# A graph network on one core: last passes with one span of 128 nodes per eight tiles, first pass with three bfloat16 parts side by side in one matmul

## What is computed

```python
h = jnp.maximum(_layernorm(x, axis=-1), 0.0)
x = x + _L0_gnn_ref(h, edge_index, edge_weight)      # segment_sum(h[src] * w, dst)
h = jnp.maximum(_layernorm(x, axis=-1), 0.0)
x = x + _L1_gnn_ref(...)                             # gate MLP per edge, summed by src
h = jnp.maximum(_layernorm(x, axis=-1), 0.0)
x = x + _L2_gnn_ref(h, edge_weight1, src, dst)       # edge softmax over dst, summed by dst, elu
h = jnp.maximum(_layernorm(x, axis=-1), 0.0)
x = x + _L3_gnn_ref(h, edge_weight, edge_index)      # segment_sum(x[src] * w, dst), twice
```

## Time and profile before

| | us |
|---|---|
| median of three timed runs | 12126.67 (12122.02 to 12133.5) |
| span of the profiled execution | 14505.6 |
| POOL busy | 9272.0 (64% of the span) |
| PE busy | 6101.2 (42%) |
| DVE busy | 4404.3 (30%) |
| ACT busy | 3763.8 (26%) |

### The profile page before, as it was taken

How to read it: one execution, slowest core, us unless ns; L and a number is a source line. 1 busy time by engine, 2 the same in 40 slices (tenths; PEclk the granted TensorE clock), 3 DMA queues, 4 the chain that set the end, 5 groups by cost and what they waited for, 6 DMA issues and landing times. The chain is left out here.

```text
span 14505.6 us, 217117 instructions
## 1 busy us (share of the span) xinstructions
PE 6101.2 (42%) x41742; PEld 4794.2 (33%) x41743; DVE 4404.3 (30%) x18474; ACT 3763.8 (26%) x13496; POOL 9272.0 (64%) x8348
## 2 busy tenths in 40 slices
PE   4444444444555555552333333233333333333333
PEld 2222122123444444442333333233333333333333
DVE  4444444445444444443111111211111111111111
ACT  2444444443222222221111111111111111111111
POOL 5555555555888888884666666566666666666665
DMA  4333333334455555542111111111111111111111
GB/s 115 101 102 100 97 96 95 94 96 66 62 61 61 61 61 62 61 61 47 16 16 16 16 16 16 20 16 16 16 16 16 16 22 16 16 16 16 16 16 21
DMA packets 805018, 671.16 MB, mean 46 GB/s; under 512 B 417876, under 2 KB 663828, under 8 KB 802727
## 3 DMA queue, kind: packets, MB, share of 16 engines
q0 software_dynamic: 452736, 234.14, 14.8%
q1 hardware_dynamic: 349659, 430.53, 11.3%
q10 hardware_dynamic: 2588, 6.12, 0.1%
HBM read 562.94 MB, written 107.13 MB: 46 GB/s over the span
## 5 line engine op out<-in xcount | busy, mean ns | idle before, releaser
L725 POOL DMA_INDIRECT table<-table,idx x4992 | 4900.3, 982 | 3003.1 <-issue 1544.4
L801 PE MATMUL psum_acc<-table 128*128 128x48 f32 (+1 forms) x12288 | 2854.8, 416 | 5083.8 <-DVE acc L765 2683.5
L801 PEld LDWEIGHTS psum_acc<-table 128*128 128x128 f32 x12288 | 2697.3, 329 | 5241.3 <-issue 5241.3
L1071 POOL DMA_INDIRECT sums<-rows,idx x1664 | 2620.6, 1575 | 577.2 <-issue 435.1
L504 POOL DMA_INDIRECT rows<-table,idx x1668 | 1689.8, 1013 | 1593.6 <-ACT idx L554 1109.8
L775 DVE TENSOR_TENSOR table<-iota,dstf 128x512 f32 x1536 | 1063.9, 693 | 2852.3 <-remote 1462.0
L732 ACT CAST idx<-srow 128x4 int32 (+1 forms) x1266 | 243.2, 193 | 6337.6 <-DVEq L783 4122.5
L765 DVE TENSOR_TENSOR acc<-acc,psum_acc x1539 | 311.8, 203 | 3547.7 <-remote 2403.7
L693 PE MATMUL psum_acc<-parts,onehot 128*128 128x48 bf16 x6144 | 338.4, 215 | 1633.2 <-DVE onehot L637 1504.7
L992 PE MATMUL psum_exp<-table,onet 128*128 x6144 | 431.8, 219 | 1384.6 <-DVE onet L915 1141.0
L743 ACT ACTIVATE table<-table,w 128x48 f32<-128x48 f32 x3328 | 840.9, 323 | 12.0 <-DMA table<-table,idx 12.0
(11 more groups left out here) (183 smaller groups left out, 7772.8 us busy)
## 6 DMA issues: line engine op xcount, KB each, us to landing
drow<-rows_dram SPq DMA_DIRECT2D x832, 128.0 KB
lrow<-in_logit_rows SPq DMA_DIRECT2D x416, 256.0 KB
table<-table,idx POOLq DMA_INDIRECT x4992
srcrow<-rows_dram SPq DMA_DIRECT2D x416, 128.0 KB
hid_dram<-hid SPq DMA_DIRECT2D x416, 96.0 KB
hid<-hid_dram SPq DMA_DIRECT2D x416, 96.0 KB
rows<-table,idx POOLq DMA_INDIRECT x1668
sums<-rows,idx POOLq DMA_INDIRECT x1664
```

The costliest lines, as they stand in the source:

```text
L725: pool.indirect_dma_start(out=ring[:, u, 0:cols], out_offset=None, in_=src_table, in_offset=bass.IndirectOffsetOnAxis(ap=idx[:, u:u + 1], ...
L801: last = nc.tensor.matmul(psum_acc[:, ds(win & 1, 1), 0:cols].rearrange("p r c -> p (r c)"), hot[:, j % 2, u, :], ring[:, j * G + u, 0:col ...
L1071: pool.indirect_dma_start(out=sums[c], out_offset=bass.IndirectOffsetOnAxis(ap=idx[:, slot:slot + 1], axis=0), in_=rows[:, slot, 0:CS], in ...
```

## The change

1. In `light_pass` the windows go. Groups have eight tiles (`LT`), and each group has one span of 128 nodes that begins at the smallest destination of the group (`bases`), wherever that lies. If a group's destinations reach over more than 128 nodes, the whole pass is run again with spans moved by 128 (`rounds`, computed on the chip). For this graph the widest group of 1,024 edges reaches over less than 128 nodes, so `rounds` is 1.
2. The operands of the matmul change places: the scaled tile is stationary (48 or 49 columns) and the one-hot matrix moves (128 columns), so sums come out transposed, features in partitions. They are added to `acc_t` [49, 12,672], and at the end of each pass PE turns all 98 blocks back with a multiplication by an identity, in batches of ten that ACT copies out of PSUM.
3. The scaling moves from four ACT instructions per four tiles to one DVE instruction per eight tiles. ACT only stages row numbers. The ring holds 64 tiles, `hot` has four buffers, and DVE adds the sum of two groups before.
4. In `first_pass` the three parts lie side by side in one matmul: 4 in place of 12 for each product. DVE sums the three parts with one more instruction per window, and the eight instructions of the dots become a product and a reduction.

```diff
+LT = 8
+LB = 8
+LAG = 2
+HOTS = 4
+BATCH = 10
...
-                                nv.tensor_tensor(acc[:, ds(k, 1), 0:cols].rearrange("p b c -> p (b c)"), acc[:, ds(k, 1), 0:cols].rearrange("p b c -> p (b c)"),
-                                                 psum_acc[:, 0, 0:cols], ALU.add).then_inc(s_added, 1)
+                                nv.tensor_reduce(out=added[:, :], in_=psum_acc[:, 0, 0:PARTS * cols].rearrange("p (q c) -> p c q", q=PARTS),
+                                                 axis=X_AXIS, op=ALU.add).then_inc(s_summed, 1)
...
+                                dve.wait_ge(s_summed, win)
...
-                            for u in range(G):
-                                last = nv.tensor_tensor_reduce(out=dots[:, u, :], in0=rows[:, j % RING * G + u, C:C0], in1=pq[:, u, :], scale=1.0,
...
+                            dve.wait_ge(s_dotted, g + 1)
+                            nv.tensor_reduce(out=adaptg[:, :], in_=dots[:, :, :], axis=X_AXIS, op=ALU.add).then_inc(s_free, 1)
...
+                                pool.wait_ge(s_picked, done + (j + 1))
+                                pool.sem_inc(s_seen, 1)
+                                for u in range(j * LT, (j + 1) * LT):
...
+                            for j in range(0, LB, 2):
+                                act.wait_ge(s_ready, done + (j + 2))
+                                nc.scalar.copy(idx_light[:, j * LT:(j + 2) * LT], srow[:, ds(i * LU + j * LT, 2 * LT)]).then_inc(s_staged, 2)
...
+                        nc.scalar.copy(total[:, b * BATCH * cols:(b * BATCH + n) * cols], psum_mlp[b % 2][:, 0:n * cols]).then_inc(s_back, 1)
...
+                    nv.memset(column, 0.0).then_inc(s_clear, 1)
...
+                                dve.wait_ge(s_landed_light[j], done * (16 * LT // LB) + 16 * LT)
+                                nv.tensor_tensor(ring[:, j * LT:(j + 1) * LT, 0:cols], ring[:, j * LT:(j + 1) * LT, 0:cols],
+                                                 weights[:, ds(i * LU + j * LT, LT)].unsqueeze(2).to_broadcast([P, LT, cols]),
+                                                 ALU.mult).then_inc(s_ready, 1)
+                                keep(done, j, late[j], s_kept)
...
+                    pe.wait_ge(s_kept, pe.snap(done_reg[pe]) + (LAG * (order + 1) + 1))
+                    pe.sem_inc(s_seen, 1)
+                    for b in range(BATCHES):
```

More of the change, by code:

```diff
@@ L389, in _ @@
                 link(nv.tensor_copy(trash[:, :], int_a[:, 1 + NBW:2 + NBW]))
+                link(nv.tensor_scalar(ident[:, :], iota[0:CS, 0:CS], node[0:CS, 0:1], None, ALU.is_equal))
+                link(nv.tensor_reduce(out=rounds[:, :], in_=counts, axis=X_AXIS, op=ALU.max))
+                link(nv.tensor_scalar(rounds[:, :], rounds[:, :], 1.0, None, ALU.add))
                 link(nv.tensor_scalar(far[:, :], node[:, :], -BIG, None, ALU.mult))
@@ new lines, in gnn_kernel, with light_rounds @@
+        late_regs = [nc.vector.alloc_register(f"light_late{j}") for j in range(LAG)]
+        moves_reg = nc.vector.alloc_register("light_moves")
+        picks = [psum_acc[:, 0, :], psum_acc[:, 1, :], psum_exp[0][:, :], psum_exp[1][:, :]]
+        BATCHES = -(-NB // BATCH)
+        def light_rounds(eng, order):
+            if order == 0:
+                eng.reg_mov(done_reg[eng], 0)
+            eng.load(rounds_reg[eng], rounds[0:1, 0:1])
+            return eng.snap(rounds_reg[eng], min_val=1, max_val=NB)
@@ L719, in _ @@
                 def _(pool):
-                    with pool.Fori(0, TURNS) as i:
-                        for j in range(GB):
-                            pool.wait_ge(s_idx, i * GB + (j + 1))
-                            pool.sem_inc(s_seen, 1)
-                            for u in range(j * G, (j + 1) * G):
-                                pool.indirect_dma_start(
-                                    out=ring[:, u, 0:cols], out_offset=None, in_=src_table,
-                                    in_offset=bass.IndirectOffsetOnAxis(ap=idx[:, u:u + 1], axis=0)).then_inc(s_landed_rows[j], 16)
+                    times = light_rounds(pool, order)
@@ L729, in _ @@
                 @block.scalar
                 def _(act):
[L731 to L745 removed]
+                    times = light_rounds(act, order)
@@ L784, in _, with keep @@
-                    keep(dve.snap(wn_dve), s_flushed)
+                        dve.reg_mov(moves_reg, 0)
+                    for late in late_regs:
+                        dve.reg_mov(late, NPAD)
+                    def keep(done, j, base, s_made):
+                        room = column[:, ds(base, P)]
+                        dve.wait_ge(s_kept, done + (j + 1 + LAG * order))
+                        dve.wait_ge(s_picked, done + (j + 1 + LB - LAG))
+                        nv.tensor_tensor(room, room, picks[(j - LAG) % HOTS][0:cols, 0:P], ALU.add).then_inc(s_made, 1)
@@ L786, in _ @@
+                    dve.reg_add(moves_reg, moves_reg, 1)
+                    dve.wait_ge(s_moved, dve.snap(moves_reg))
+                    dve.sem_inc(s_seen, 1)
+                    done = dve.snap(done_reg[dve])
+                    for j in range(LAG):
+                        keep(done, j, dve.snap(late_regs[j], min_val=0, max_val=NPAD), s_kept)
                 @block.tensor
                 def _(pe):
+                    times = light_rounds(pe, order)
                     if order == 0:
-                        pe.sem_inc(s_picked, 2)
@@ new lines, in _ @@
+                    with pe.Fori(0, times):
+                        with pe.Fori(0, LTURNS):
+                            done = pe.snap(done_reg[pe])
+                            for j in range(LB):
+                                pe.wait_ge(s_ready, done + (j + 1 + LB))
+                                for u in range(LT):
+                                    last = nc.tensor.matmul(picks[j % HOTS][0:cols, 0:P], ring[:, j * LT + u, 0:cols], hot[:, j % HOTS, u, :],
+                                                            start=(u == 0), stop=(u == LT - 1))
+                                last.then_inc(s_picked, 1)
+                            pe.reg_add(done_reg[pe], done_reg[pe], LB)
```

210 lines of the change are left out of this document (118 added, 92 removed).

## The result

The change makes the kernel slower: 12507.51 us (12502.66 to 12516.66, 4 runs) against 12126.48 (4 runs), a ratio of 1.0314 (95% interval 1.0301 to 1.0327), +381 us. The record said 12,450 (12,120 to 12,790) and gave "slower by over 0.2%" a chance of 0.81. The profiled execution after spans 12500.9 us and its timed run was 12502.66, so nothing has to be taken off here, where 2379 us had to be before.

The account below looks back on a forecast made before the run. The prediction took POOL, at 1.25 us per gather, to set the pace of all five passes. 12126.67 + 138 (turning back) + 165 (port hold) + 8 (starts) + 20 (first pass) = 12,458, stated as 12,450 us, range 12,120 to 12,790.

Parts of the forecast that it names:

- The reading of the profile: All five passes: without the recorder POOL sets the pace, 1.25 us per gather; stalls of 2337 us aren't in timed runs.
- The rival in which the late answers are real: Last passes: PE's late answers are real and the 0.30 us the recorder's, so 11,170 us; chance 0.14.
- What is removed: Last passes: window loops, 304 of 512 one-hots and ACT's scaling lie beside POOL's 1.25 us per tile; gain 0.
- Turning back: Ends of the last passes: 98 blocks turned back while POOL is idle, 46 us per pass, +138 for three.
- floor of 134: Turning back, three last passes: can hardly go below 3 x 44.7 = 134 us, from setup's 98 similar matmuls.
- ceiling of 276: Turning back, three last passes: twice as much, 276 us, if PE ran at the lower of its clock levels.
- Port hold: Last passes: gathers starting during longer DVE one-hots and scalings end late; 122 us per pass against 67, +165 for three.
- the rival in which they always miss: Last passes: DVE instructions always miss POOL's starts, 175 us given back, total 12,100 to 12,150; chance 0.05.
- the formula: Last passes: a DVE instruction of length D costs POOL (D - 0.12)^2 / (2 x 1.25) us on average.
- Starts: Pass starts and setup: loading `rounds` ahead of each pass, small instructions and four DMAs more; 0 to 20 us, +8.
- First pass: First pass: PE's gain is hidden by POOL, DVE's longer work slightly exceeds POOL's pace; +20 us (0 to 62).
- The rival in which it falls off that pace: First pass: staging three groups ahead doesn't even out one- and two-window groups; +341 instead of +20, 12,770 us; chance 0.10.

Follow-up runs that it names:

- the run with before's last passes: The kernel before with only the diff's first pass changed (three parts side by side, one reduction, product over 384 columns); ratio to before 1.0004, +5 us.

## Why the prediction was right, and where a term was off

**The reading of the profile** held. The time is set by POOL, at 1.25 us per gather that isn't held and 1.88 per scatter of the L1 pass, and the stalls of before's profile weren't in the time. This rested on a sum that came within 42 us of the median; a profile of the same loops without stalls now shows it. The rival in which the late answers are real (11,170 us) is refuted.

**What is removed gave nothing**, as said. PE's matmul instructions in a last pass fell from 4088 to 3312, ACT's busy time from 475 to 20 us, and POOL's 1664 steps stayed.

**Turning back**: +138 predicted. From the last gather of a pass to the next stage's first gather (or the end) it was 58.6, 16.2 and 18.3 us in the run with before's last passes, and is 99.8, 58.9 and 61.3: +41.2, +42.7, +43.0, so +127. The term was a little large: the blocks took 39.4 to 42.0 us where setup's, of 64 columns and another shape, took 44.7. The floor of 134 that I called hard was therefore none, and the ceiling of 276 for the lower clock level was far off: at a granted clock of 0.50 the block takes 42.0 us.

**Port hold**: +165 predicted, (322 + 17) - 148 = +191 measured. The mean over phases fits the one-hot well (0.51 us per group said, 0.516 measured, 322 / 624), although the phase isn't random: 408 of the gathers held start 0.5 to 0.6 us into the one-hot, so this agreement is partly luck. The 624 one-hots hold 602 gathers, which refutes the rival in which they always miss. The scaling was overestimated (0.08 against 0.03), because 139 of the gathers that start during it do so within its first 0.045 us and go free, which the formula doesn't know; and so were the holds before (67 us per pass against 49).

**Starts**: +8 predicted with 20 as the upper bound, 41 measured. This is the step that failed. "The longer memset of `acc_t` lies under the 80 us that POOL's ring of 64 lasts" looked at what POOL waits for by semaphores, and not at the port that it shares with DVE, which I had priced for the one-hots alone. The copy behind the memset holds the gather that is running until the memset and the copy are done: 34.7 us. The other 6 are setup (the first gather at 130.02, was 125.09) and one more after the scatters.

**First pass**: +20 predicted (0 to 62), between -7 and +16 measured. POOL's pace covers the longer DVE work. The rival in which it falls off that pace is refuted.

The terms as measured, 127 + 191 + 41 + 0 = 359, agree with the 357.6 us between the two spans (12500.9 and 12143.3). The timed difference is 381; the 22 us between are about what chips and runs differ by (the interval of the ratio alone is 16 us to each side, and the medians of before lie up to 43 us apart). The forecast of +331 was nearer than its terms, by luck: a port hold 26 too small and starts 33 too small against 11 and 20 too large.

**Still open**: what made the one recorded execution of before stall (no other profile here does); why chains of eight scalar one-hots hold gathers in the changed kernel (behind the scaling above all, but a little without it too) and never by more than 0.14 us in the kernel before. Chains in the changed kernel that start at the same moments of POOL's steps as in the kernel before weren't tried.

## What to carry to other kernels

Where one engine issues gathers back to back, every other engine's work is free only as far as it doesn't share a port with it: list the DVE instructions with two inputs in SBUF, and the copies, and give one input a place in PSUM. To make one input a scalar removed the holds in the kernel before and made them worse in the changed one, so it has to be tried. The two together were worth 1.7% in the kernel before, while the change, which took a fifth of PE's instructions and nearly all of ACT's work out of the last passes, gained nothing by it. Look at what is queued *behind* a long harmless instruction, too. And before believing stalls in a profile, add up the time without them and hold it against the timed runs.

## What the runs showed of the hardware

- A one-hot, scaling or running maximum on DVE with two SBUF inputs holds a gather that starts during it until 0.82 us behind its own end (602 gathers by the one-hots of one kernel); with one input in PSUM the running maximum holds none (0 of 186).
- A gather that starts within the first 0.045 us of the scaling goes free (139 of 139); of those that start later with over 0.3 us of it to go, all 47 are held.
- With a copy of 0.19 us behind a memset of 10.62 us, a gather took 12.43 us, and another was held already 0.63 us before its memset began; in the other order none was held.
- A block of 196 float32 matmul instructions of 48 columns took 39.4 to 42.0 us at a granted clock of 0.50 to 0.54, no more than a block of 196 with 64 columns in setup (44.7 us at a granted clock of 1.00).
- Scalar one-hots (one SBUF tile each) in an unbroken run of DVE instructions behind a two-input one held gathers that started 0.5 us into them by 0.68 us on average; the same instructions in another kernel, in chains of four or eight, held none by more than 0.14.
